# A vision tower on one core: the last two image pairs finished in one interleaved passage, the start reordered

## The reference

```python
h = tok(x)                         # patches @ W.T: 64 images x 196 tokens x 192
q, k, v = silu(h@Wq), silu(h@Wk), silu(h@Wv)          # 12 heads of 16
energy = (q @ k.T) * where(n >= m, exp(log_slope * (n - m)), 0)
a = layernorm((energy @ v) * sigmoid(h@Wg1@Wg2) @ Wo)
h = layernorm(h + a)
xn = rmsnorm(h);  tok_ = l2norm(xn);  sl = l2norm(slots) * scale
logits = sl @ tok_.T                                  # per image, slots x tokens
y = softmax(logits, tokens) @ xn                      # dispatch
y = gelu(y @ fc1[s] + b1[s]) @ fc2[s] + b2[s]         # weights of slot s
h = layernorm(h + softmax(logits, slots).T @ y)       # combine
```

## Time and profile before

| what | us |
|---|---|
| three runs | 1175.16, 1176.07, 1183.46 |
| median | 1176.07 |
| the profiled execution | 1180.63 |
| its span, first to last instruction | 1178.9 |
| from the start to the first matmul | 13.02 |
| pair 31's last attention matmul to phase 2's first matmul | 862.29 to 897.70 |

### The profile page before, as it was taken

The page is one execution under the profiler, slowest core; times in us unless marked ns, Lnnn a source line. Parts: engine busy times, 40 slices in busy tenths (PEclk is TensorE's granted clock), DMA queues, the critical chain, the costliest instruction groups (busy, mean ns, idle before and its releaser), DMA issues.

```text
span 1178.9 us, 35548 instructions
## 1 busy us (share of the span) xinstructions
PE 1086.4 (92%) x13226; PEld 859.6 (73%) x13226; DVE 843.1 (72%) x2115; ACT 725.9 (62%) x1713; POOL 636.2 (54%) x974
## 2 busy tenths in 40 slices
PE   4889999999999999999999999999989999997553
PEld 4678888888888888888888888888875556555331
DVE  4578888888888888888888888888861222223996
ACT  4357777777777777777777777777743111110666
POOL 5357666566666666676666666766532000001664
PEclk9789999999999999999999999999989999998555
DMA  4411111211111112111111121111083999995886
GB/s 157 191 65 53 56 56 54 86 67 65 54 54 54 54 54 89 66 63 54 54 54 54 56 90 65 61 54 54 14 339 118 421 423 424 423 423 161 250 261 179
DMA packets 50994, 158.48 MB, mean 134 GB/s; under 512 B 5658, under 2 KB 31664, under 8 KB 38644
## 3 DMA queue, kind: packets, MB, share of 16 engines
q1 hardware_dynamic: 33352, 145.11, 33.5%
q10 hardware_dynamic: 17600, 12.78, 3.5%
HBM read 132.25 MB, written 25.62 MB: 134 GB/s over the span
## 4 chain that ended last, share of the span: by engine, by line
PE 83%; DVE 9%; ACT 3%; issue 2%; DVEq 1%; SPq 1%; DMA 1%; POOL 0%; ACTq 0%; POOLq 0%
PE ps L1054 9%; PE ps L1056 7%; PE ps L1055 7%; PE ps L1143 7%; PE ps L1176 6%; PE ps L1365 6%; PE ps L1221 4%; PE ps L1384 4%; PE ps L1076 3%; PE ps L1127 3%; PE ps L1128 3%; DVE res L1023 2%; PE ps L1113 2%; PE ps L1212 2%; PE ps L1389 2%; PE ps L1398 2%
## 5 line engine op out<-in xcount | busy, mean ns | idle before, releaser
L432 POOL TENSOR_TENSOR xl<-x_sb,xh 128x392 fp32r<-128x392 f32 x192 | 194.1, 1041 | 9.2 <-ACT xh L584 9.1
L889 DVE TENSOR_TENSOR p_sb<-ps,dec 98x1568 f32<-98x1568 f32 x96 | 172.0, 1792 | 26.6 <-PE ps L1143 23.8
L485 POOL TENSOR_TENSOR hTl<-hT,hTh 128x392 fp32r<-128x392 f32 x64 | 66.5, 1039 | 140.0 <-ACT hTh L689 104.5
L724 ACT ACTIVATE hg<-ps 128x768 f32<-128x768 f32 x32 | 26.0, 811 | 147.5 <-PE ps L1389 147.5
L837 DVE SCALAR_TENSOR_TENSOR t<-t,rstd,hb 98x192 f32<-98x192 f32 x128 | 85.5, 709 | 24.0 <-POOL rstd L496 24.0
L1015 DVE COPY y2st<-ps 128x192 f32<-128x192 f32 x32 | 11.5, 358 | 120.4 <-PE ps L1365 120.4
L535 POOL CAST pickb<-pick 128x128 fp32r (+1 forms) x32 | 9.4, 293 | 150.4 <-PE ps L1389 150.4
L1176 PE MATMUL ps<-p_sb,vpad 98*32 98x98 f32 x3072 | 87.4, 255 | 0.9 <-DVE p_sb L889 0.9
L523 POOL TENSOR_TENSOR Cn<-Ec,crec 98x256 f32<-98x256 f32 x32 | 20.5, 640 | 123.7 <-DVE crec L926 123.7
L741 ACT ACTIVATE o_sb<-res,nb,rstd 98x192 f32<-98x192 f32 x128 | 59.6, 536 | 43.7 <-DVE nb L1038 43.0
L1176 PEld LDWEIGHTS ps<-p_sb,vpad 98*32 98x32 f32 x3072 | 66.2, 112 | 25.9 <-issue 13.6
(11 more groups left out here) (216 smaller groups left out, 3451.4 us busy)
## 6 DMA issues: line engine op xcount, KB each, us to landing
x_sb<-in_xT SPq DMA_DIRECT2D x32, 1176.0 KB, 5.4
w1v<-in_fc SPq DMA_DIRECT2D x32, 1152.0 KB, 10.6
w2v<-in_fc SPq DMA_DIRECT2D x32, 1152.0 KB, 13.1
h_dram<-h SPq DMA_DIRECT2D x32, 294.0 KB
h2r<-h_dram SPq DMA_DIRECT2D x32, 294.0 KB
out<-o_sb ACTq DMA_DIRECT2D x32, 294.0 KB
comb_dram<-cst SPq DMA_DIRECT2D x32, 98.0 KB, 5.1
cbuf<-comb_dram SPq DMA_DIRECT2D x32, 98.0 KB, 3.9
```

Source lines behind the costliest of these rows:

```text
L432: pool.tensor_tensor(xl[:, k], x_sb[:, k], xh[:, k].bitcast(F32), ALU.subtract)\
L889: dve.tensor_tensor(dst, src, rate.unsqueeze(2).to_broadcast([T, 4, 2, TOK]), ALU.mult)\
```

## The change

**The start.** Loads: the slopes have a semaphore of their own, so the decays no longer wait for W. Keys', queries' and gate's first weights follow the images at once, then the values', and the other ten loads go behind the second pair's images. ScalarE makes 12 decays, rounds the first images, and then makes the last four decays. The low part of the first images is made half on GpSimd and half on VectorE (`xl0_rdy`), and the causal cut moves behind the first `low_h`. VectorE splits keys' and queries' weights first and the values' and gate's in `value_weights` after `summed_h`. TensorE opens with 18 idle products as soon as the identity is there, and waits for `w_split` at 4, then 8, then 12. The slots are turned in step 1 instead of at the end of step 0.

**The end.** The steps NP and NP+1 are gone and `phase1` has lost the flag a. In their place each engine has a passage that finishes pairs `one` = 30 and `last` = 31 in an order written out by hand. The idle products there are 8, 6, 8, 2, 8, 4, 2, 6 and 2 in place of 8, 12, 16, 2, 6, 2, 4 and 2. On SP the store of pair 29's combine weights moves behind the load of ring buffer 3 and the store of pair 30's h2. The loop between is as it was.

```diff
-            step(0, True, False, False, False, False, True)
-            step(1, True, True, False, False, False, True)
-            step(2, True, True, True, False, False, True)
-            step(3, True, True, True, True, False, True)
+            step(0, False, False, False, False, True)
+            step(1, True, False, False, False, True)
+            step(2, True, True, False, False, True)
+            step(3, True, True, True, False, True)
             with eng.Fori(4, NP - 1) as i:
-                step(i, True, True, True, True, True, True)
-            step(NP - 1, True, True, True, True, True, False)
-            step(NP, False, True, True, True, True, False)
-            step(NP + 1, False, False, True, True, True, False)
+                step(i, True, True, True, True, True)
+            step(NP - 1, True, True, True, True, False)
...
+            sp.dma_start(slope[:, :], log_slope.partition_broadcast(T)).then_inc(slopes_loaded, 16)
+            sp.dma_start(rslope[:, :], row_slope).then_inc(slopes_loaded, 16)
+            sp.dma_start(wst[:, :, :], W).then_inc(first_loaded, 16)
             sp.dma_start(x_sb[:, :, :], xT[0]).then_inc(x_loaded, 16)
+            sp.dma_start(wkst[:, :, :], Wk).then_inc(qk_loaded, 16)
+            sp.dma_start(wqst[:, :, 0:D], Wq).then_inc(qk_loaded, 16)
             sp.wait_ge(gst_zeroed, 2)
-            for dst, src in loads:
-                sp.dma_start(dst, src).then_inc(loaded, 16)
+            for at in (D, D + ZL):
+                sp.dma_start(wqst[:, :, at:at + RANK], Wg1).then_inc(qk_loaded, 16)
+            sp.dma_start(wvst[:, :, :], Wv).then_inc(v_loaded, 16)
+            for row in (0, ZL, ZT):
+                sp.dma_start(gst[row:row + RANK, :], Wg2).then_inc(v_loaded, 16)
...
+            sp.wait_ge(xl0_rdy, KP // 2)
             load_x(1)
+            for dst, src in loads:
+                sp.dma_start(dst, src).then_inc(loaded, 16)
...
             load_weights(2, 2)
-            store_comb(NP - 3)
             sp.wait_ge(og_sb, 2 * NP)
             load_weights(3, 3)
             store_h2(NP - 2)
+            store_comb(NP - 3)
             store_comb(NP - 2)
...
-            split_x(0, range(KP))
-
-            pool.wait_ge(dec_exp, HX)
-            pool.affine_select(out=dec[:, :, :], in_=dec[:, :, :], compare_op=ALU.is_ge, fill=0.0, base=0,
-                               pattern=[[0, HX], [1, T]], channel_multiplier=-1).then_inc(dec_rdy, 1)
+            for k in range(KP // 2):
+                pool.wait_ge(xh_rdy, 1)
+                pool.tensor_tensor(xl[:, k], x_sb[:, k], xh[:, k].bitcast(F32), ALU.subtract)\
+                    .then_inc(xl_rdy, 1 if k < KP // 2 - 1 else KP // 2 + 1)
+
+            def causal_decays():
+                pool.wait_ge(dec_exp, HX)
+                pool.affine_select(out=dec[:, :, :], in_=dec[:, :, :], compare_op=ALU.is_ge, fill=0.0, base=0,
+                                   pattern=[[0, HX], [1, T]], channel_multiplier=-1).then_inc(dec_rdy, 1)
...
+                low_h(i, 0)
+                if at_start(i):
+                    causal_decays()
...
+            first_norm(last, 0)
+            inverse_norms(one)
+            first_norm(last, 1)
+            scaled_tokens(one)
+            token_scales(last)
+            combine_weights(one)
+            inverse_norms(last)
+            scaled_tokens(last)
+            combine_weights(last)
...
+            decays(range(H))
+            for k in range(2):
+                round_x(0, k)
+            decays(range(H, HX))
...
+            second_norm(one)
+            squares(one)
+            token_rows(one)
+            slot_inputs_kept(one - 1, 0, TOK)
+            combine_kept(one - 1, 0, True)
+            use_table(ACT.Exp)
+            slot_exponentials(one)
+            dispatch(one)
+            slot_inputs_kept(one, 5, 0)
+            token_exponentials(one)
+            squares(last)
+            token_rows(last)
+            second_norm(last)
+            combine_kept(one, 4, True)
+            slot_exponentials(last)
+            dispatch(last)
+            token_exponentials(last)
+            slot_inputs_kept(last, 5, 0)
+            combine_kept(last, 4, True)
...
+            for k in range(KP // 2, KP):
+                dve.wait_ge(xh_rdy, 2)
+                dve.tensor_tensor(xl[:, k], x_sb[:, k], xh[:, k].bitcast(F32), ALU.subtract).then_inc(xl0_rdy, 1)
+            dve.wait_ge(qk_loaded, 64)
+            dve.tensor_copy(wkh[:, :, :], wkst[:, :, :]).then_inc(w_split, 1)
             dve.tensor_copy(wqh[:, :, :], wqst[:, :, :]).then_inc(w_split, 1)
-            dve.tensor_copy(wkh[:, :, :], wkst[:, :, :]).then_inc(w_split, 1)
-            dve.tensor_copy(gw[:, :], gst[:, :]).then_inc(w_split, 1)
-            dve.tensor_copy(wvh[:, :, :], wvst[:, :, :]).then_inc(w_split, 1)
-            dve.wait_ge(w_split, 8)
-            dve.tensor_tensor(wvl[:, :, :], wvst[:, :, :], wvh[:, :, :].bitcast(F32), ALU.subtract).then_inc(w_split, 1)
+            dve.wait_ge(w_split, 6)
+            dve.tensor_tensor(wkl[:, :, :], wkst[:, :, :], wkh[:, :, :].bitcast(F32), ALU.subtract).then_inc(w_split, 1)
             dve.tensor_tensor(wql[:, :, :], wqst[:, :, :], wqh[:, :, :].bitcast(F32), ALU.subtract).then_inc(w_split, 1)
-            dve.tensor_tensor(wkl[:, :, :], wkst[:, :, :], wkh[:, :, :].bitcast(F32), ALU.subtract).then_inc(w_split, 1)
-            low = slice(ZL, GZ)
-            dve.tensor_tensor(gw[low, :], gst[low, :], gw[low, :].bitcast(F32), ALU.subtract).then_inc(w_split, 1)
-
             dve.wait_ge(parity_rdy, 2)
-            dve.wait_ge(dec_rdy, 1)
-            dve.wait_ge(tables, 3)
+
+            def value_weights():
...
+            def slots_kept():
...
+                if isinstance(i, int) and i == 1:
+                    slots_kept()
...
+                if at_start(i):
+                    value_weights()
...
+            mean_shifts(one)
+            for g, n in enumerate((slice(0, PT), slice(PT, COLS))):
+                dve.wait_ge(ogh_rdy, 2 * last + 1 + g)
+                dve.tensor_tensor(ogl[:, n], og[:, n], ogh[:, n].bitcast(F32), ALU.subtract).then_inc(ogl_rdy, 1)
+            tokens(one)
+            first_norm(last, 0)
+            token_norms(one)
+            first_norm(last, 1)
+            residual(last, 0)
+            cosine_scales(one)
+            cosines(one)
+            residual(last, 1)
+            residual_statistics(last, 0)
+            residual_statistics(last, 1)
+            slot_maxima(one)
+            tokens(last)
+            slot_sums(one)
+            shifted_logits(one)
+            token_norms(last)
+            mean_shifts(last)
+            token_sums(one)
+            cosine_scales(last)
+            cosines(last)
+            slot_maxima(last)
+            shifted_logits(last)
+            slot_sums(last)
+            token_sums(last)
...
-            pe.wait_ge(w_split, 4)
-            pe.wait_ge(pick_sum, 1)
+            pe.wait_ge(ident_st, 2)
...
+                embed(i, 0, c, e)
+                if isinstance(i, int) and i == 1:
                     slots_turned()
...
-            def last_steps(i, c):
-                if c:
-                    idle_products(0, 8)
-                    project_out(i - 1, 0)
-                token_features(i - 2)
-                if c:
-                    project_out(i - 1, 1)
-                    combine_turned(i - 3, 0)
-                    slot_inputs_turned(i - 3, 0, TOK)
-                else:
-                    idle_products(1, 6)
-                logits(i - 2)
-                idle_products(1, 12 if c else 2)
-                if c:
-                    pe.wait_ge(cb_sb, i - 2)
-                    pe.wait_ge(yT_sb, 2 * i - 4)
-                logits_turned(i - 2)
-                idle_products(1, 16 if c else 4)
-                dispatch_turned(i - 2)
+            def drain():
+                one, last = NP - 2, NP - 1
+                idle_products(0, 8)
+                project_out(last, 0)
+                token_features(one)
+                project_out(last, 1)
+                combine_turned(one - 1, 0)
+                slot_inputs_turned(one - 1, 0, TOK)
+                logits(one)
+                idle_products(1, 6)
+                pe.wait_ge(cb_sb, one)
+                pe.wait_ge(yT_sb, 2 * one)
+                logits_turned(one)
+                idle_products(1, 8)
+                dispatch_turned(one)
                 idle_products(1, 2)
-                slot_inputs(i - 2)
-                if c:
-                    pe.wait_ge(t1_rdy, 4 * i)
-                combine_turned(i - 2, 4)
-                slot_inputs_turned(i - 2, 5, 0)
+                slot_inputs(one)
+                pe.wait_ge(t1_rdy, 4 * NP)
+                slot_inputs_turned(one, 5, 0)
+                idle_products(2, 8)
+                token_features(last)
+                idle_products(2, 4)
+                logits(last)
+                combine_turned(one, 4)
```

(13 more changed lines are left out.)

298 lines of the change are left out of this document (139 added, 159 removed).

## The result

| kernel | median us | runs | lowest to highest |
|---|---|---|---|
| before | 1179.00 | 7 | 1175.16 to 1183.46 |
| changed | 1166.03 | 7 | 1162.13 to 1169.55 |

The ratio is 0.9889, with a 95% interval of 0.9864 to 0.9914: 13.0 us less, and faster by just over 1%. The forecast of 1160.6 was 5.4 too low. 2.9 of these lie in the base, since the three runs that the forecast started from had a median of 1176.07 and the seven have 1179.00. The other 2.5 are gain that didn't come (13.0 instead of 15.5).

The account below looks back on a forecast made before the run. TensorE's own pace was taken to bound both long stretches, so savings at start and finish count in full: -4.5 - 5.0 - 6.0 = -15.5 from the profiled 1180.63, less 4.56 to the median, gives 1160.6 us; range 1154 to 1169.

Parts of the forecast that it names:

- rival B: Finish: half clock throughout, idle products eat the gain, so the finish brings 0 and the kernel takes 1166.6; chance 0.17.
- A: Whole kernel: the forecast itself holds, 1154 to 1166 us; chance 0.58.
- The start, up to the scores: From kernel start to pair 0's scores: earlier image rounding and later weight splits bring scores 4.5 us earlier (2.5 to 5.4).
- Step 0 to step 1: Pair 0's last matmul to first output projection: idle gap goes, embedding at full clock; 5.0 us saved (3.0 to 5.4).
- The finish: Pair 31's last attention matmul to phase 2: three steps sum to -7.1 at full clock, -6.0 with 1.1 allowed for half clock.
- (1): Finish: ScalarE's h2 of pair 30 stands first, so pair 31's gn starts at 874.2 instead of 880.52; -6.3.
- (2): Finish, gn's start to pair 31's turned features: 5.5 us instead of 7.66; -2.2.
- (3): Finish's very end: last pair's combine weights come behind its slots' inputs and phase 2 waits for them; +1.4 (0.5 to 2.5).
- It costs nothing more: Finish: holding pair 31's squares on ScalarE some 3 us behind pair 30's Ec adds nothing, as TensorE's features aren't earlier.
- Rival C: Step 0: VectorE and GpSimd exclude each other, rows_of_v start some 2.1 us later, kernel 1162.7; chance 0.12.
- Rival D: Step 1: VectorE's chain sets the pace, so the start brings only 5 and the finish 2, kernel 1169; chance 0.10.
- Rival E: Finish: pair 31's h2 waits for pair 30's store; slower than before from 15 us on; kernel 1190, chance 0.03.

Follow-up runs that it names:

- E4: Changed kernel without the 18 idle products with which TensorE opens; median 1166.94 us, ratio 0.9911 to the kernel before.
- E12: The kernel before, unchanged, run once more for its trace, one execution; 1175.43 us.
- E5: Changed kernel with the slots turned and kept at the end of step 0 again; median 1169.25 us, ratio 0.9927 to the kernel before.
- E10: Changed kernel with ScalarE's h2 of pair 30 late again, behind the combine weights' copy; median 1169.88 us, ratio 0.9940 to the kernel before.
- E7: Changed kernel with the last pair's combine weights ahead of its slots' inputs; median 1164.37 us, ratio 0.9879 to the kernel before.
- E3: The changed kernel as it is, run again on another chip; median 1167.33 us, ratio 0.9909 to the kernel before.
- E1: Kernel before with only the start's part of the change, old finish; median 1169.57 us, ratio 0.9942 to the kernel before.
- E2: Kernel before with only the finish's part of the change, old start; median 1173.29 us, ratio 0.9964 to the kernel before.
- E11: Changed kernel with last pair's combine weights first, pair 30's h2 stored before loads, pair 31's squares and features earlier; 1160.47 us, ratio 0.9862 to before.
- E8: As E7, with 2 + 3 idle products in the gaps around the last turnings; median 1163.52 us, ratio 0.9880 to the kernel before.
- E9: Changed kernel without the finish's 38 idle products behind the first eight; median 1166.65 us, ratio 0.9912 to the kernel before.
- E6: Changed kernel with pair 30's h2 stored ahead of the load of ring buffer 3; median 1165.92 us, ratio 0.9899 to before.

## Why the prediction was right where it was, and what was off

The direction and the range (1154 to 1169) held, and so did most of the steps. The number alone would not tell the forecast from rival B: 1166.03 lies at the very edge of A (1154 to 1166), and B gave 1166.6. The traces do, since B has the finish bring nothing, and it is 6.6 us shorter in the profile at full clock. It is partly luck that the three terms sum to 15.4 over two executions of each, where 15.5 was forecast: they are -3.8, -6.0 and -5.6, and the second has 1 us in it from the first profile's clock.

- **The start, up to the scores: -4.5.** Against the same profile -4.94, over two executions of each -3.8. The steps are there one by one: first chunk 10.98 (10.9), end of the embedding 18.30 (18.3), keys' second parts 22.16 (21.6), scores 26.51 (27). The 0.7 for uncovered value weights was not needed: TensorE's rows of v went at 23.43 without waiting for them. The 18 opening products bring nothing (E4), as was counted. One reading of the rows was off and without effect: the four splits of keys' and queries' weights, put at 3 us beside GpSimd, took 4.2 there; in the changed kernel, with GpSimd idle, they took 1.8 (13.94 to 15.76).
- **Step 0 to step 1: -5.0.** Over the stretch from the scores to the first output projection -7.2 against the first profile and -4.7 against E12, -6.0 in the mean. 5.0 had been reckoned for the gap and for the embedding behind it at full clock, and that is what both profiles show: from the last attention matmul to the projection 8.78 and 8.49 before, 3.65 now (the gap of 2.98 in both, and E5 when it is put back). What the prediction didn't see is that pair 0's attention in the profile of before ran partly at half clock, by chance of that execution. -2.0 of the -12.1 stand there, between the scores and the last attention matmul of pair 0 (43.41 to 36.45).
- **The finish: -6.0.** (1) -6.3 for h2: gn came 12.21 after the attention instead of 18.29, -6.1, and E10 gives 4.2 of it back by moving one group. (2) -2.2 to the turned features: 7.66 became 5.60, -2.1. (3) +1.4 for the combine weights at the end: 9.52 became 11.02, +1.5, and E7 gets 1.1 of it back. The sum of -7.1 was 6.6 in the profile. The 1.1 allowed for the clock was not needed there, but E3 lost 2.1 to it; the mean is -5.6, and that 1.1 is the mean of what the two executions lost (0 and 2.1) is luck.
- **What was mis-sized: the sum left out what comes behind the finish.** The text took phase 2's start as at half clock before and after alike. Over the two executions of each kernel that stage got 1.2 longer. Over all profiles it took 4.67 or 4.68 in two of the three with the old finish and 6.23 to 7.77 in six of the seven that have the changed kernel's end as it is. And phase 3 took 0.9 longer in each kernel with the new start, E1 among them, and not in E2, though its code is the same. The traces show where. VectorE's sum for the sixth pair comes 0.4 later, behind a short idle time in which it waited for nothing that the profile shows, and each further round of its loop takes 0.1 more. That sum before, 14.50 behind phase 3's first matmul, and in the changed kernel, 14.91 behind it:

```profile
1098.31 0.96 DVE L1023 TENSOR_TENSOR res<-ps,h2r 98x768 f32<-98x768 f32 x1
```

```profile
1080.89 0.96 DVE L1088 TENSOR_TENSOR res<-ps,h2r 98x768 f32<-98x768 f32 x1 [0.36 <-issue]
```

Together with 0.2 in the pair loop these 2.3 are nearly all of the missing 2.5. Why VectorE stands still there was not tested, and it stays open.

- **"It costs nothing more" for pair 31's squares** was right in size and not in its reason. VectorE waited 3.70 for them. The sentence looked at TensorE's features, while the squares lead over VectorE and GpSimd (invn) to the scales of the cosines. In the changed kernel these were done at 871.87 and TensorE's logits at 871.56, so the squares held Lt back by 0.3 only; that is read from the trace, and no run moves the squares alone. E11 moves squares and features both and has Lt 1.1 sooner, and its passage was no shorter than E7's.
- **Rival B**: half clock through the whole finish came in no profile with the products. Part of it came in E3 and E4, at a price of 2.1 each, and in none of the other six profiles with the same finish up to there (the changed kernel's own, E2 and E5 to E8: 5.59 and 5.60 from gn to the features). The Trainium skill (TensorE: Matmul & The Clock Gate, "HAM oscillation — how this bites in real kernels") says that gaps put TensorE back to half rate and that keeping it fed holds the full rate. E9 agrees in direction (0.50 from 864 without the products, and the lowest mean grant in all its executions), and so does E8 in its one profile; E3, fed as the changed kernel is, was at 0.56 and 0.50 from 866 to 872.
- **Rival C**: the exclusion of VectorE and GpSimd is there. The low part of gw on VectorE took 1.05 for its 16 rows, beside the end of GpSimd's hTl and its next xl (from 22.06); before, with GpSimd idle, it took 0.35:

```profile
22.50 0.35 DVE L782 TENSOR_TENSOR gw<-gst,gw 16x192 fp32r<-16x192 f32 x1
```

The step that did not hold is that TensorE would wait: its rows of v went at 23.43 without waiting for it.

- **Rival D**: the start alone brings 6.8 (4.7 to 9.0), not 5, and is not given back by VectorE's chain: the pair loop is 0.2 longer (0.5 in E1), not 4.
- **Rival E**: the wait exists (1.50, and 1.97 in E7), far from the 15 that it would have needed. "Each us later is a us for the whole kernel" did not hold for these 1.5: without them phase 2 begins 28.83 after the attention all the same (E6).

## What to carry to other kernels

When a kernel's time hangs on stretches of some tens of us at its ends, take the marks of those stretches from two or three executions before pricing anything: here they moved by 3.8 us in the start and 2.1 in the finish with the same instructions, and the granted clock moved with them. Follow each saving to the stage behind it (the first pair of phase 2, the round through DRAM ahead of phase 3), since this is where 2.1 of 15.5 us went. The two moves in the finish that paid were changes of place of one instruction group (h2, which holds back a buffer, and the combine weights, which phase 2 waits for). A long wait in the trace only names a candidate: the 3.70 for the squares and the 1.50 for the store stood beside other work that was nearly as late.
